# The product of the input with B on GpSimd for 4 of the 16 state indices, in a selective-scan kernel

## The reference

```
xs = stack([x0, x1, reversed x0, reversed x1])      # 4 directions over 4096 tokens, 256 channels
dts, Bs, Cs = split(x_proj of xs)                   # R = 8, N = 16, N = 16
delta = softplus(dt_proj of dts + bias)
def step(h, t):                                     # h: 256 channels x 16 state indices
    h = exp(d_t * A) * h + (d_t * x_t) * B_t
    return h, einsum('bkdn,bkn->bkd', h, C_t)
```

## Time and profile before

| | |
|---|---|
| median of 3 executions | 26486.41 us (26484.9 to 26491.68) |
| span of the profiled execution | 26472.5 us, 13.9 us under that median |
| VectorE busy | 25249.3 us, 95% of the span |
| TensorE busy | 20800.8 us, 79% |
| GpSimd busy | 16821.7 us, 64% |
| ScalarE busy | 16551.4 us, 63% |
| mean granted TensorE clock | 0.957 of full speed |

### The profile page before, as it was taken

How to read it: one execution, slowest core, us unless ns; L and a number is a source line. 1 busy time by engine, 2 the same in 40 slices (tenths; PEclk the granted TensorE clock), 3 DMA queues, 4 the chain that set the end, 5 groups by cost and what they waited for, 6 DMA issues and landing times.

```text
span 26472.5 us, 271753 instructions
## 1 busy us (share of the span) xinstructions
PE 20800.8 (79%) x48516; PEld 8224.1 (31%) x49344; DVE 25249.3 (95%) x28655; ACT 16551.4 (63%) x31677; POOL 16821.7 (64%) x7108
## 2 busy tenths in 40 slices
PE   7778778778777777877877877787778778778777
PEld 3333333333333333333333333333333333333333
DVE  9998998998999899899899899969999998998998
ACT  6665665665666566666566566656666665665665
POOL 5765765775677477577577567707775765775775
PEclk9999999999999999999999999999999999999999
DMA  0000000000000000000000000010000000000000
GB/s 15 7 0 17 7 0 16 0 7 16 1 7 4 16 7 1 16 0 7 16 0 7 10 7 7 0 58 1 7 4 13 7 0 16 0 7 16 1 7 7
DMA packets 53095, 222.41 MB, mean 8 GB/s; under 512 B 4384, under 2 KB 4512, under 8 KB 45600
## 3 DMA queue, kind: packets, MB, share of 16 engines
q1 hardware_dynamic: 51744, 209.22, 2.1%
HBM read 125.31 MB, written 83.89 MB: 8 GB/s over the span
## 4 chain that ended last, share of the span: by engine, by line
issue 48%; DVE 34%; PE 7%; ACT 7%; DVEq 3%; POOL 0%; DMA 0%; ACTq 0%; another core or an unknown queue 0%; POOLq 0%; SPq 0%
DVE WK L584 21%; DVE WK L567 7%; PE PS L361 3%; DVE WK L561 2%; ACT PS L787 2%; DVE WK L558 2%; PE PS L474 1%; PE PS L487 1%; ACT YP L771 1%; DVEq L577 1%; DVEq L579 1%; DVE X L645 1%; ACT CS L780 1%; ACT WK L762 1%; PE PS L349 1%
## 5 line engine op out<-in xcount | busy, mean ns | idle before, releaser
L937 POOL TENSOR_TENSOR HC<-WK,CS 128x1024 f32<-128x1024 f32 x6144 | 14824.7, 2415 | 7065.8 <-DVE WK L584 5702.7
L584 DVE TENSOR_TENSOR_SCAN WK<-PS,CARRY,WK 128x512 f32<-128x512 f32 x12288 | 15593.2, 1269 | 114.0 <-ACT PS L787 99.5
L787 ACT ACTIVATE PS<-WK,ANEG 128x512 f32<-128x512 f32 x12288 | 8452.0, 691 | 8013.6 <-DVE WK L584 8009.6
L361 PE MATMUL PS<-HC,KC 128*128 128x512 f32 x24576 | 12368.4, 628 | 648.9 <-ACT YP L771 641.3
L567 DVE TENSOR_TENSOR WK<-WK,PS 128x512 f32<-128x512 f32 x12288 | 8055.4, 656 | 46.6 <-DVE WK L584 45.0
L349 PE MATMUL PS<-PARTS,SEL 128*128 128x512 bf16 x11616 | 3727.7, 398 | 4715.8 <-DVE WK L567 4560.8
L361 PEld LDWEIGHTS PS<-HC,KC 128*128 128x128 f32 x24576 | 4849.4, 200 | 5367.6 <-issue 3879.4
L349 PEld LDWEIGHTS PS<-PARTS,SEL 128*128 128x128 bf16 x12288 | 1155.0, 99 | 9761.2 <-DVE WK L567 8332.6
L780 ACT ACTIVATE CS<-PS 128x512 f32<-128x512 f32 x6144 | 3586.9, 584 | 379.2 <-PE PS L349 358.4
L924 POOL TENSOR_TENSOR WK<-WK 128x1024 f32<-128x1024 f32 x384 | 911.4, 2373 | 2416.4 <-DVE WK L555 2416.4
L767 ACT ACTIVATE CARRY<-WK 128x2 f32<-128x2 f32 x5376 | 1012.8, 188 | 0.0
(11 more groups left out here) (114 smaller groups left out, 11580.2 us busy)
## 6 DMA issues: line engine op xcount, KB each, us to landing
gates<-WK SPq DMA_DIRECT2D x96, 512.0 KB, 3.0
X<-gates SPq DMA_DIRECT2D x12, 4096.0 KB, 12.8
X<-hidden SPq DMA_DIRECT2D x20, 2048.0 KB, 8.0
hidden<-WK SPq DMA_DIRECT2D x96, 256.0 KB, 2.0
X<-in_x SPq DMA_DIRECT2D x8, 2048.0 KB, 8.8
YP<-hidden SPq DMA_DIRECT2D x4, 2048.0 KB, 9.2
out<-WK SPq DMA_DIRECT2D x32, 256.0 KB, 2.0
W<-w SPq DMA_DIRECT2D x3, 2004.5 KB, 12.4
```

What stands on the lines that cost most here:

```text
L361: mm = pe.matmul(YB[:, h], ident, HC[:, slot, h], start=(n == 0), stop=(n == N - 1))
L584: dve.tensor_tensor_scan(c.run(HS[n % RING][:, h]), c.run(DAB[:, h]), c.run(DBX[n % 2][:, h]), CARRY[:, n, h:h + 1], ALU.mult, ALU.add).th ...
L787: act.activation(DAB[:, h], DELTA[par][:, h], ACT.Exp, scale=ANEG[:, a:a + 1])\
L937: pool.tensor_tensor(HC[:, n % RING], HS[n % RING], both(CS[:, n % RING]), ALU.mult).then_inc(s["readout_ready"], 1)
```

## The change

For n in 3, 6, 11 and 14 the input `DX * B` is no longer made by VectorE (two instructions of 128x512) but by GpSimd (one of 128x1024), into a buffer of its own, `DBXP`. GpSimd has no access to PSUM here, so ScalarE first copies B of that index from PSUM to a new SBUF tile `BS`. ScalarE does this two steps ahead, GpSimd makes the product three steps ahead, behind its readout of n - 3. The waits of TensorE, VectorE and GpSimd are counted anew to match.

```
+POOL_N = (3, 6, 11, 14)
+POOL_AHEAD = 3
...
+        DBXP = sb("DBXP", [P, DH, CH])
+        BS = sb("BS", [P, CH])
...
 # TensorE, before it spreads B of n + 2
-                        pe.wait_ge(s["input_ready"], st * DH + DH)
+                        if n in POOL_N:
+                            pe.wait_ge(s["b_copied"], c.pool_inputs(n) + 1)
+                        else:
+                            pe.wait_ge(s["input_ready"], c.own_inputs(n) + DH)
...
 # VectorE
-                        if n + 1 < N or nxt:
+                        if (n + 1 < N or nxt) and n + 1 not in POOL_N:
...
-                        dve.wait_ge(s["input_ready"], st * DH + (h + 1))
+                        if n not in POOL_N:
+                            dve.wait_ge(s["input_ready"], c.own_inputs(n) + (h + 1))
+                        elif h == 0:
+                            dve.wait_ge(s["pool_input"], c.pool_inputs(n) + 1)
...
-                        dve.tensor_tensor_scan(c.run(HS[n % RING][:, h]), c.run(DAB[:, h]), c.run(DBX[n % 2][:, h]),
+                        dbx = DBXP[:, h] if n in POOL_N else DBX[n % 2][:, h]
+                        dve.tensor_tensor_scan(c.run(HS[n % RING][:, h]), c.run(DAB[:, h]), c.run(dbx),
...
 # ScalarE, behind the two decays of step n
+                    if n + 2 in POOL_N:
+                        act.wait_ge(s["b_ready"], st + 3)
+                        if prev or POOL_N.index(n + 2):
+                            act.wait_ge(s["pool_input"], c.pool_inputs(n + 2))
+                        act.activation(BS[:, :], BB[:, n % 2], ACT.Copy).then_inc(s["b_copied"], 1)
...
 # GpSimd, behind the readout of step n
+                    m = n + POOL_AHEAD
+                    if m in POOL_N:
+                        pool.wait_ge(s["b_copied"], c.pool_inputs(m) + 1)
+                        pool.wait_ge(s["dx_ready"], c.i + 1)
+                        if POOL_N.index(m):
+                            pool.wait_ge(s["state_ready"], (c.step + POOL_N[POOL_N.index(m) - 1]) * DH + DH)
+                        elif prev:
+                            pool.wait_ge(s["state_ready"], (c.step - N + POOL_N[-1]) * DH + DH)
+                        pool.tensor_tensor(DBXP[:, :], DX[par], both(BS[:, :]), ALU.mult).then_inc(s["pool_input"], 1)
```

More of the change, by code:

```diff
@@ L41 @@
 POOL_SLOTS = {8: "error", 10: "log1p"}
+POOL_N = (3, 6, 11, 14)
+POOL_AHEAD = 3
+OWN_N = tuple(n for n in range(N) if n not in POOL_N)
 MERGE = 4
@@ L173, in program @@
             "b_ready", "c_ready", "decay_ready", "c_copied", "input_ready", "state_ready", "carry_ready",
-            "readout_ready", "ysum_done", "y_merged",
+            "readout_ready", "ysum_done", "y_merged", "b_copied", "pool_input",
             "on_half", "on_mean", "on_cent", "on_sq", "on_sum", "on_var", "on_log", "on_rstd", "on_norm", "gated", "oproj",
@@ L209, in __init__, with own_inputs, pool_inputs @@
                 self.turned = img.scan(NCH) + NCH
+            def own_inputs(self, n):
+                return self.i * (len(OWN_N) * DH) + sum(m < n for m in OWN_N) * DH
+            def pool_inputs(self, n):
+                return self.i * len(POOL_N) + sum(m < n for m in POOL_N)
             def tokens(self):
```

## The result

The changed kernel takes 26,261.74 us (median; 26,250.08 to 26,267.7), the kernel before 26,485.9: ratio 0.9915, 95% interval 0.9901 to 0.9929. It is 0.85% faster. I had forecast 27,000 us, slower, and held the faster side for less likely (0.30). The time lies inside the stated range, beside the rival "one instruction" (26,180 us); the range reached down to it only because it took in the let-in case, to which I had given 0.27.

What follows compares the result with a forecast made beforehand. VectorE was taken as the bound. Per chunk, -0.8 us with "delta" let in and +3.5 held, half each, gave +1.35, times 384 = +520 us: 27,000 us, range 26,170 to 27,830.

Steps and rivals of the forecast that it cites:

- one instruction: Rival: "delta" waits only for GpSimd's running instruction and is let in almost every time; -310 us, 26,180 us, chance 0.27.
- let-in case: "delta" gets in after readout 11, product 14 then waits for it; -0.8 us a chunk, -310 us, chance 0.27.
- What 'delta' meets: Between scans 8 and 14, "delta" meets a GpSimd queue and may be held until it empties, as in six of twelve images.
- the draw: Each chunk's "delta" is held or let in, half each: -0.8 or +3.5 us, on average +1.35 us a chunk.
- Removed: Eight VectorE inputs of 0.575 us fewer in each chunk: -4.6 us a chunk, 1.77 ms in all.
- wait of scan 14: If "delta" is let in, product 14 ends late and scan(14, h0) starts 2.6 us later in the chunk.
- "input": If "delta" is let in, "input" comes later into readout 12 and waits 1.0 instead of 0.4 us: +0.6.
- Waits of scans for ScalarE: At n = 5, scan(5, h0) waits 0.83 us for ScalarE in half of the chunks: +0.4 us on average.
- all else unseen: Allowance for more waits on ScalarE and TensorE's slower clock behind merges: 0.2 us a chunk, bounds 0 and 0.6.
- Half way: Rival: "delta" is let in, then "input" is passed over behind readouts 12 and 13; +1.5 us a chunk, 27,070 us.
- Hidden anyway: Rival: GpSimd's product is shorter or its queue has a gap, and "delta" slips in; 25,100 us, chance 0.02.
- ScalarE late: Rival: four more waits cost ScalarE 0.3 us each on decays; +0.5 ms on top of any other case.

Runs made afterwards that it cites:

- fresh run: Changed kernel with GpSimd's additions at the image end all put behind ScalarE's last square, so that GpSimd pauses first: 26,309.75 us (one run).
- halves from n = 11 on: Changed kernel with GpSimd's readouts of n = 11 to 15 and product of n = 14 each made as two 128x512 instructions: 26,465.67 us (one run).
- three indices: Changed kernel with products only for n = 3, 6, 11, VectorE making the input of n = 14 itself again: 26,293.42 us, ratio to before 0.9931.
- no products: Changed kernel with all four GpSimd products cut to one column, all waits and ScalarE's copies kept: 25,446.22 us, ratio to before 0.9609.
- wide additions: Changed kernel with GpSimd's eight 128x512 additions at the image end made as four of 128x1024: 26,258.75 us (one run).
- long run: Changed kernel with every GpSimd instruction from the readout of n = 8 on made as two of 128x512: 27,845.64 us (one run).
- the same with the spreads first: Kernel with indices 3, 6, 8, 10, TensorE's first sum of a chunk put behind the two spreads of the next step: 25,280.23 us.

## Why the prediction was wrong

**The step that failed is "What 'delta' meets".** It read a true thing in the trace, VectorE passed over by an unbroken run in six of twelve images, and carried its share over to "delta" as it stood. But the eight L956 that I counted there follow eight L953 without a pause, so at the image end VectorE arrives in the 13th instruction of a run and not in the 5th. In the chunk it arrives in the 7th, and there 1 of 372 was passed over and not every second. The runs in the order of that number, counted since GpSimd's last pause:

| VectorE comes in instruction | kernel and place | passed over |
|---|---|---|
| 4th, or as the 5th begins | fresh run, image end | 0 of 12 |
| 7th | changed kernel, "delta" | 1 of 372 |
| 8th | halves from n = 11 on | 2 of 372 |
| 8th | three indices | 9 of 372 |
| 9th, two of them of one column | no products | 12 of 372 |
| 11th, three of them wide | wide additions, image end | 2 of 12 |
| 13th | kernel before, image end | 6 of 12 |
| 13th or 14th | long run, "delta" | 255 of 372 |
| 10th to 14th | indices 3, 6, 8, 10, "delta" | 2 of 372 |
| 11th to 15th | the same with the spreads first | 0 of 372 |

The last two rows break the order. In both "round" got in during the run, and counted from the GpSimd instruction that waited for it "delta" comes in the 8th, where 2 and 0 of 372 fit. So a count that starts anew at a pause or when VectorE gets in fits all rows; that was read off after the runs, and no run was made to test it. Nor do the runs tell a run of many instructions from one of many short ones: where a half or more were passed over, all were of 128x512, and no wide run of 13 without an entry of VectorE occurred. What is shown by experiment is that a pause put into the run brings 6 of 12 to 0 of 12, and that thirteen short instructions in the place of seven wide ones bring 1 of 372 to 255. Elapsed time doesn't explain it: the 7th and the 13th of the chunk come at the same 15 us behind the start of the run. The form of VectorE's instruction, an arrival out of a pause at the start of GpSimd's instruction, and short instructions just around "delta" were each tried, and none of them by itself brings more than 2 of 372. I took the one place that I had for a law of queues; the share of a long run did not hold for a shorter one.

**With one instruction in place of the draw, the sum holds.** Predicted for "let in" were -0.8 us a chunk; the spans give (26,265.9 - 26,472.5) / 384 = -0.54. Term by term, a chunk, from the rows above against the earlier trace rows:

- Removed: 4.6 us by the pitch, as forecast (the plain steps lost exactly their inputs).
- "delta" +0.72 (1905 - 1190 ns by the groups) and the wait of scan 14 +1.69 (650.4 us / 384): 2.4 where 2.6 were forecast.
- "input" +0.45 (2022 - 1574), forecast 0.6.
- Waits of scans for ScalarE: (429.6 - 99.5) / 384 = +0.86, forecast 0.4. **This term was mis-sized.** By steps, in the order of the scans in the trace, scan 5 waits 117.6 us in all, only in the turned directions: +0.31, the 0.4 that I had forecast. But scan 6 waits 225.0 where it waited 99.5 before (+0.33), and scan 13 waits 73.6, all in the first direction (+0.19). I walked through n = 4 and 5 and stopped. VectorE makes no input during step 5, so it comes to scan 6 two inputs sooner, while what ScalarE and TensorE have to do behind the merge has not become less. The trace before showed that wait (1.04 us at just that scan); I had it only as a bound of what I couldn't see. Why scan 13 waits was not looked into; like scan 5 it has no input in front of it any more.
- Idle time before inputs: (148.8 - 46.6) / 384 = +0.27, most of it waits for TensorE (91.0 us); forecast 0.2 with all else unseen.

The sum of these is -4.6 + 4.0 = -0.6. It comes near the -0.8 partly because errors cancel: "delta" with scan 14 and "input" cost 0.35 less than forecast, the other waits 0.5 more.

The rule of the Trainium skill ("SBUF — State Buffer", "Who interferes with whom"), that whoever issues first has the shared pair for the whole instruction and the other is blocked meanwhile, agrees with 371 of 372 deltas here. In the long run it does not: 255 of 372 deltas waited for GpSimd instructions that began after them. The measurement decides.

**The rivals.** "Half way" is out: no "input" was passed over in any run. "Hidden anyway" was right in what it would be worth (25,100 us), and the kernel with 3, 6, 8, 10 is that case made on purpose (25,128). "ScalarE late" came true in part: scans 6 and 13 cost 0.5 us a chunk beyond the forecast, some 200 us and not 500.

## What to carry to other kernels

Work moved to an engine with 64% load is not free where its new instructions fall among the old ones: count, for each stretch between two waits, what the helper must do before the bound engine may go on. Four products at 3, 6, 8, 10 took 5.1% off, the same four at 3, 6, 11, 14 only 0.85%, and of these the last gained nothing. Keep GpSimd from running a dozen short instructions without a pause just before VectorE needs an instruction with two operands in SBUF; and when a frequency is taken from another place of the trace, ask what differs there before it is put into the sum.

## What the runs showed of the hardware

- VectorE's instructions with two SBUF operands wait for the end of GpSimd's running instruction and are then usually let in (371 of 372 deltas, which then end 1.1 us behind it). Behind a long unbroken GpSimd run they are passed over until it ends: 255 of 372 as the 13th or 14th of a run of 128x512 instructions (9.6 to 10.5 us), 1 of 372 as the 7th of wide ones. Why the length of the run matters stays open.
- Once passed over, VectorE never got in before the run's end, in any run; GpSimd's instructions kept their length meanwhile.
- The mean granted TensorE clock was 0.957 of full speed before, 0.933 with 3, 6, 11, 14 and 0.959 with 3, 6, 8, 10. By steps of the chunk the loss is not behind the merges (steps 4 and 5: 0.81 and 0.75 before, 0.90 and 0.71 after) but in steps 14 and 15: 0.98 and 0.93 before, 0.82 and 0.64 after, 0.97 and 0.90 with 3, 6, 8, 10. In step 14 TensorE stands still for 3.3 us on average where it was 1.3 us, since it waits for VectorE's input of n = 15, whose second half now comes behind the late scan 14 and the longer "input". The granted clock in the trace is either 1.0 or 0.5 of full speed (2.4 or 1.2 GHz); the figures above are means. In the chunk shown above TensorE waits 4.70 us for that second half, until 2797.08, and the granted clock is 1.00 from 2788 to 2794 us and 0.62 in the next 6.
